# The row sums of the attention weights: once per chunk from a running total on VectorE

## The chip, the cores and the metric

One core of a Trainium2 chip runs the whole program: two transformer layers on a batch of two. Its engines are TensorE (PE; PEld is its weight load), VectorE (DVE), ScalarE (ACT), GpSimd (POOL) and SyncE (SP), which here only starts DMAs. The metric is the device time of one execution in microseconds (us). Three runs of the kernel before had a median of 2285.57 us.

## The reference

```python
# x: (2, 1024, 512) float32; 16 heads of 32 columns; layer 0, then layer 1
xn = layernorm(x)
x = x + attention(xn) + feed_forward(xn)

# attention of one head, causal:
scores = (q_rotated @ k_rotated.T) * 32 ** -0.5        # (1024, 1024), keys after the query masked
pattern = softmax(scores, axis=-1)                     # exp(s - row max) / row sum of these
heads = pattern @ v
out = heads @ Wo.T

# feed-forward: silu(xn @ Wgate.T) * (xn @ Wup.T), then @ Wdown.T
#   2048 hidden columns in layer 0, 1408 in layer 1
```

The row sums are the sums over the keys of the unnormalised weights, exp(score - shift).

## The kernel before

**Tiling.** The 16 heads go in 4 groups of 4. In each layer a group is one turn: a loop body run three times (region `turn0` in layer 0, `turn1` in layer 1) and a fourth, separately written turn (`tail0`, `tail1`). With a batch of two that makes 16 turns: six long turns (layer 0, which carry two pairs of feed-forward chunks), six short turns (layer 1, which carry one pair) and two tails of each layer. A turn has these stages: natural scores (`nat`), from which VectorE takes row maxima; `shift`; the transposed scores and their exponentials; then projection, rotation and DMAs for the next group.

**Scores and weights.** The queries go in two chunks of 512, the keys in blocks of 128. A set is one (chunk, key block): sets 0 to 3 belong to chunk 0, sets 4 to 11 to chunk 1. The last four sets of each chunk are masked and narrow: 512, 384, 256, 128 columns. For each set and each of the four heads, `st` makes scores S<-QS,KS on TensorE (with a second small matmul for the mask) in one of two banks, and ScalarE writes exp of it to `pr`, which has room for two sets. `pv` multiplies the four heads' values with the weights into bank O, and `sums` multiplies a matrix of ones with the same weights into bank E: four matmuls each, on four groups of 32 columns. After a chunk's last `sums`, `heads` copies O and E to SBUF (`heads`, `denom`). Then VectorE takes the reciprocal in two halves (`recip`), scales (`scaled`), ScalarE and GpSimd split the result in a high and a low part (`ah`, `al`), and `wo` multiplies it by the output weights; `add_wo` adds to the residual.

**Order.** `weighted()` writes out the sets: scores of two heads, `pv` of the set before, scores of two heads, `sums` of the set before. `turn()` merges these pieces by hand-written numbers (`FILL`, `LATE`) with pieces of the feed-forward (gate, up, down). The first chunk has none between its sets. Every engine walks the same list of steps and takes its own part of each, in order. So where a step stands in the list is its place in every engine's queue, and a wait at the head of a queue holds all that is behind it. Waits count semaphores: `a_exp` for exponentials, `p_pv` for the weights' last reader, `a_heads` for the copied O and E.

**Where the steps of the second chunk stand.** In a long turn `recip` half 0 follows set 5's first scores and `pv` 4, half 1 and `scaled` follow set 5's last scores, and `wo` stands after `pv` 8. In a short turn both halves and `scaled` stand behind `pv` 5, between the first and the second pair of set 6's scores, and `wo` ahead of set 8. In layer 0's tail half 0 stands ahead of set 6, half 1 and `scaled` ahead of set 7, `wo` behind `pv` 6.

## Time and profile before

| | us |
|---|---|
| three runs, median (lowest to highest) | 2285.57 (2283.03 to 2285.79) |
| profiled execution, span from the first to the last instruction | 2287.4 |
| TensorE busy in it | 2116.6 (93%) |
| VectorE busy | 1159.1 (51%) |
| ScalarE busy | 739.0 (32%) |
| GpSimd busy | 680.0 (30%) |
| mean granted TensorE clock | 0.979 |

The profile has no other time for its own execution than the span. It is 1.8 us above the median of the runs. A busy TensorE is not one at its peak, since matmuls are pipelined and their ends are modelled; starts are better to read than ends. A granted clock of 1.00 is 2.4 GHz, 0.50 is 1.2 GHz.

### The profile page before, as it was taken

What the parts mean: (1) busy time and instruction counts of PE and PEld (TensorE: products, weight loads), DVE (VectorE), ACT (ScalarE), POOL (GpSimd) and SP (SyncE); (2) the same over time, 40 slices, a digit from 0 to 9 for tenths busy, and PEclk for the clock granted to TensorE, in tenths of its full rate; (3) what the DMA queues carried; (4) which work ended last, traced back from release to release, by engine and by line L of the source; (5) the groups of instructions that cost most, each with busy time, mean ns of one, the idle gap of its engine ahead of it and who ended that gap; (6) DMA issues with size and microseconds to landing.
All of it is one profiled execution on the core that took longest, in us unless ns stands there. A gap on an engine that the chain in (4) does not pass through costs nothing.

```text
span 2287.4 us, 35555 instructions
## 1 busy us (share of the span) xinstructions
PE 2116.6 (93%) x11200; PEld 1390.8 (61%) x11200; DVE 1159.1 (51%) x1946; ACT 739.0 (32%) x1357; POOL 680.0 (30%) x428
## 2 busy tenths in 40 slices
PE   4999999999889999999969999999998999999997
PEld 3756656566475656576557566665765756475764
DVE  5534636355445546464356255462645546382733
ACT  3242242423323333423322423324233232424232
POOL 3314323142221414142323142331422314041523
PEclk9999999999999999999979999999998999999998
DMA  3303103141021303040123031130411303030403
GB/s 134 79 29 93 42 22 82 32 111 43 19 73 44 79 28 96 10 115 29 51 101 95 11 93 43 41 85 11 120 34 37 79 20 97 10 96 10 124 21 127
DMA packets 72439, 141.10 MB, mean 62 GB/s; under 512 B 9328, under 2 KB 26736, under 8 KB 71152
## 3 DMA queue, kind: packets, MB, share of 16 engines
q1 hardware_dynamic: 72304, 139.25, 21.9%
q8 instruction: 91, 1.49, 0.3%
q14 instruction: 44, 0.36, 0.1%
HBM read 75.77 MB, written 4.19 MB: 35 GB/s over the span
## 4 chain that ended last, share of the span: by engine, by line
issue 73%; POOL 25%; POOLq 1%; DMA 0%; SPq 0%; ACT 0%
POOL hl L716 5%; POOL swapped L722 4%; POOL pr L728 3%; POOL wgl L693 3%; POOL wul L693 2%; POOL wdl L693 2%; POOL wqkl L693 2%; POOL al L732 2%; POOL raw L709 1%; POOL wol L693 1%; DMA tt<-in_wdown_dram 0%; POOL QS L701 0%; POOLq L715 0%; POOLq L711 0%; POOLq L725 0%
## 5 line engine op out<-in xcount | busy, mean ns | idle before, releaser
L629 ACT ACTIVATE pr<-S 128x512 f32<-128x512 f32 (+3 forms) x768 | 342.2, 489 | 316.5 <-PE S L958 217.2
L847 DVE TENSOR_TENSOR xres<-D,xres 128x512 f32<-128x512 f32 x352 | 242.3, 688 | 370.2 <-PE D L879 364.0
L716 POOL TENSOR_TENSOR hl<-tt,hh 128x512 fp32r<-128x512 f32 x108 | 138.8, 1285 | 872.8 <-ACT hh L653 872.5
L955 PE MATMUL S<-QS,KS 98*128 98x512 f32 (+2 forms) x768 | 267.4, 411 | 19.8 <-ACT pr L629 11.0
L955 PEld LDWEIGHTS S<-QS,KS 98*128 98x128 f32 x768 | 145.1, 192 | 188.3 <-ACT pr L629 165.5
L653 ACT CAST hh<-tt 128x512 fp32r<-128x512 f32 x108 | 67.0, 620 | 488.8 <-DVE tt L861 488.8
L821 DVE TENSOR_REDUCE mp<-S 128x1 f32<-128x128 f32 (+3 forms) x384 | 176.7, 484 | 71.7 <-PE S L937 61.2
L837 DVE RECIPROCAL denom<-denom 128x256 f32<-128x256 f32 x64 | 109.0, 1729 | 186.4 <-ACT denom L636 186.4
L879 PE MATMUL G<-xh,wgh 128*128 128x512 f32 x432 | 180.0, 417 | 19.1 <-issue 13.8
L879 PE MATMUL D<-wdh,hh 128*128 128x512 f32 x432 | 183.8, 426 | 4.1 <-DVE xres L847 3.0
L879 PE MATMUL G<-xh,wgl 128*128 128x512 f32 x432 | 178.2, 412 | 0.0
L879 PE MATMUL U<-xh,wul 128*128 128x512 f32 x432 | 177.3, 410 | 0.0
L879 PE MATMUL G<-xl,wgh 128*128 128x512 f32 x432 | 176.2, 408 | 0.0
L879 PE MATMUL U<-xh,wuh 128*128 128x512 f32 x432 | 174.5, 404 | 0.0
L879 PE MATMUL U<-xl,wuh 128*128 128x512 f32 x432 | 174.4, 404 | 0.0
L879 PE MATMUL D<-wdl,hh 128*128 128x512 f32 x432 | 172.0, 398 | 0.0
L879 PE MATMUL D<-wdh,hl 128*128 128x512 f32 x432 | 171.3, 397 | 0.0
L972 PE MATMUL O<-pr,vh 128*32 128x512 f32 (+3 forms) x1536 | 163.6, 498 | 0.1
L979 PE MATMUL E<-pr,ones 128*32 128x512 f32 (+3 forms) x1536 | 163.4, 497 | 0.0
L858 DVE SCALAR_TENSOR_TENSOR tt<-tt,G 128x512 f32<-128x512 f32 x108 | 73.3, 678 | 125.0 <-ACT tt L647 125.0
L821 DVE TENSOR_REDUCE mp<-O 128x1 f32<-128x512 f32 (+1 forms) x192 | 122.9, 640 | 19.5 <-PE O L934 9.5
L934 PE MATMUL S<-KS,QS 96*128 96x256 f32 (+2 forms) x384 | 121.7, 363 | 9.2 <-DMA QS<-pr 7.5
(145 smaller groups left out, 3794.1 us busy)
## 6 DMA issues: line engine op xcount, KB each, us to landing
KS<-pr SPq DMA_DIRECT2D x192, 128.0 KB, 2.3
QS<-pr SPq DMA_DIRECT2D x192, 128.0 KB, 2.3
raw<-in_wgate_dram SPq DMA_DIRECT2D x29, 512.0 KB, 4.2
raw<-in_wup_dram SPq DMA_DIRECT2D x28, 512.0 KB, 3.7
raw<-in_wdown_dram SPq DMA_DIRECT2D x28, 512.0 KB, 3.5
raw<-in_wqk_dram SPq DMA_DIRECT2D x18, 512.0 KB, 3.5
vh<-val SPq DMA_DIRECT2D x16, 512.0 KB, 3.9
val<-in_x_dram SPq DMA_DIRECT2D x6, 1024.0 KB, 11.0
```

The source lines that it names most:

```text
L629: act.activation(pr[:, (i * HG + h) % 8, skip:W], S[h % 2][:, skip:W], ACT.Exp, scale=SCALE) \
L693: return pool.tensor_tensor(flat(lo), src[:, 0:SIZE[kind]], flat(hi).bitcast(F32), ALU.subtract)
L716: pool.tensor_tensor(hl[:, fc, :], tt[:, (blk * nfc + fc) % 2, :], hh[:, fc, :].bitcast(F32), ALU.subtract) \
L722: pool.tensor_tensor(sw, sw, trig[:, 1, (t % NC) * W:(t % NC + 1) * W], ALU.mult).then_inc(sem["g_sin"], 1)
L821: dve.tensor_reduce(mp[:, h * RT + qb, part:part + 1], NB[(h * len(NAT) + u) % 4][:, 0:w_], AX.X, ALU.max) \
L837: dve.reciprocal(denom[:, half], denom[:, half]).then_inc(sem["v_recip"], 1)
L847: dve.tensor_tensor(xres[:, rt, :], d[:, :], xres[:, rt, :], ALU.add).then_inc(sem["v_dfree"], 1)
L879: ins = pe.matmul(dst, a, b_, start=i == 0, stop=i == len(seq) - 1)
L934: ins = pe.matmul(s[:, 0:wide], QS[0:STACK, h, qb * P:(qb + 1) * P], KS[0:STACK, h, k0:k0 + wide], start=True, stop=not masked)
L955: ins = pe.matmul(s[:, first:W], KS[0:SHIFT, h, kb * P:(kb + 1) * P], QS[0:SHIFT, h, c * W + first:(c + 1) * W], start=True, stop=not masked)
L972: pe.matmul(O[h * DH:(h + 1) * DH, skip:W], vh[:, kb, h * DH:(h + 1) * DH], pr[:, (i * HG + h) % 8, skip:W], start=kb == 0, stop=kb == TPC ...
L979: ins = pe.matmul(E[h * DH:(h + 1) * DH, skip:W], ones[:, :], pr[:, (i * HG + h) % 8, skip:W], start=kb == 0, stop=kb == TPC * (c + 1) - 1)
```

## The change

`sums` is made once per chunk instead of once per set. VectorE keeps a running total `acc` of the four heads' weights. A chunk's first set is the total itself (set 0, whose exponentials are written straight into `acc`) or is copied into it (set 4); each other set is added by one instruction over all four heads (`acc`, eight additions and one copy per turn). TensorE then multiplies the ones with `acc`, 512 columns per head, behind the chunk's last set. `pv` now counts for itself (`p_pv`), the sums have a semaphore of their own (`p_sums`), and an exponential waits for three things: its scores, `pv` of two sets before, and the total's addition of two sets before. `acc` takes the space of two buffers that are unused at that time (`swapped`, `xn`).

```diff
     st = [[[("st", 0, h) for h in two] for two in ((0, 1), (2, 3))]]
     for i in range(1, len(SETS) + 1):
         scores = [("st", i, h) for h in range(HG)] if i < len(SETS) else []
-        now = [scores[:2] + [("pv", i - 1)], scores[2:] + [("sums", i - 1)]]
+        now = [scores[:2] + [("pv", i - 1)], scores[2:]]
+        if i > 1:
+            now[0].append(("acc", i - 1))
         c, kb = SETS[i - 1]
         if kb == TPC * (c + 1) - 1:
-            now[-1].append(("heads", c))
+            now[-1] += [("sums", c), ("heads", c)]
         st.append(now)
     return st
 
     "nat": {"p_nat": 1, "v_max": 1},
     "shift": {"v_chain": 2, "v_m": 1, "p_shift": 1, "v_shift": 1, "d_shift": 32},
     "st": {"p_st": 1, "a_exp": 1},
-    "pv": {},
-    "sums": {"p_pv": 1},
+    "pv": {"p_pv": 1},
+    "acc": {"v_acc": 1},
+    "sums": {"p_sums": 1},
     "heads": {"a_heads": 1},
     "recip": {"v_recip": 1},
     "scaled": {"v_heads": 1, "a_ah": 1, "g_al": 1},
...
-        swapped = sb("swapped", [P, 2, W])
+        acc = sb("acc", [P, HG, W])
+        swapped, xn = acc[:, 0:2, :], acc[:, 2:4, :]
...
             at = n.turns * (2 * PAIRS[1]) + (2 * j + fc)
             return bass.ds(at, 1)
 
+        def weights(i):
+
+            return pr[:, i * HG % 8:i * HG % 8 + HG, :] if i else acc
+
         def proj_bank(n, t):
 
             return S[t % 2] if n.region[:4] == "open" else NB[t]
                 c, kb = SETS[i]
                 skip = max(0, kb - TPC * c) * P
                 act.wait_ge(sem["p_st"], n("p_st", 1))
-                act.wait_ge(sem["p_pv"], n("p_pv"))
-                act.activation(pr[:, (i * HG + h) % 8, skip:W], S[h % 2][:, skip:W], ACT.Exp, scale=SCALE) \
+                later = -1 if h >= 2 else 0
+                act.wait_ge(sem["p_pv"], n("p_pv", later if i else 0))
+                if i:
+                    act.wait_ge(sem["v_acc"], n("v_acc", later if i > 1 else 0))
+                else:
+                    act.wait_ge(sem["p_sums"], n("p_sums"))
+                act.activation(weights(i)[:, h, skip:W], S[h % 2][:, skip:W], ACT.Exp, scale=SCALE) \
                     .then_inc(sem["a_exp"], 1)
 
             def heads_(n, c):
-                act.wait_ge(sem["p_pv"], n("p_pv"))
+                act.wait_ge(sem["p_sums"], n("p_sums"))
                 act.wait_ge(sem["g_al"], n("g_al"))
                 act.copy(heads[:, :], O[:, :])
                 act.copy(denom[:, :], E[:, :]).then_inc(sem["a_heads"], 1)
                 dve.wait_ge(sem["p_shift"], n("p_shift", 1))
                 dve.tensor_copy(mt[:, :], E[0:2 * HG * RT, 0:P]).then_inc(sem["v_shift"], 1)
 
+            def accumulate(n, i):
+                c, kb = SETS[i]
+                skip = max(0, kb - TPC * c) * P
+                dve.wait_ge(sem["a_exp"], n("a_exp", -2 if i < len(SETS) - 1 else 0))
+                if i == 1:
+                    dve.wait_ge(sem["p_pv"], n("p_pv", -1))
+                total_, now = acc[:, :, skip:W], weights(i)[:, :, skip:W]
+                if kb:
+                    dve.wait_ge(sem["v_acc"], n("v_acc"))
+                    ins = dve.tensor_tensor(total_, total_, now, ALU.add)
+                else:
+                    dve.wait_ge(sem["p_sums"], n("p_sums"))
+                    ins = dve.tensor_copy(total_, now)
+                ins.then_inc(sem["v_acc"], 1)
+
             def recip(n, c, k):
                 dve.wait_ge(sem["a_heads"], n("a_heads"))
                 half = slice(k * W // 2, (k + 1) * W // 2)
 
                 pe.wait_ge(sem["a_exp"], n("a_exp", -2 if i < len(SETS) - 1 else 0))
                 for h in range(HG):
-                    pe.matmul(O[h * DH:(h + 1) * DH, skip:W], vh[:, kb, h * DH:(h + 1) * DH],
-                              pr[:, (i * HG + h) % 8, skip:W], start=kb == 0, stop=kb == TPC * (c + 1) - 1)
-
-            def sums(n, i):
-                c, kb = SETS[i]
-                skip = max(0, kb - TPC * c) * P
+                    ins = pe.matmul(O[h * DH:(h + 1) * DH, skip:W], vh[:, kb, h * DH:(h + 1) * DH],
+                                    weights(i)[:, h, skip:W], start=kb == 0, stop=kb == TPC * (c + 1) - 1)
+                ins.then_inc(sem["p_pv"], 1)
+
+            def sums(n, c):
+                pe.wait_ge(sem["v_acc"], n("v_acc"))
                 for h in range(HG):
-                    ins = pe.matmul(E[h * DH:(h + 1) * DH, skip:W], ones[:, :], pr[:, (i * HG + h) % 8, skip:W],
-                                    start=kb == 0, stop=kb == TPC * (c + 1) - 1)
-                ins.then_inc(sem["p_pv"], 1)
+                    ins = pe.matmul(E[h * DH:(h + 1) * DH, :], ones[:, :], acc[:, h, :], start=True, stop=True)
+                ins.then_inc(sem["p_sums"], 1)
 
             def wo_(n, c, i):
                 if c == 0 and i == 0:
```

VectorE's queue in a short turn, after the first chunk: `acc<-pr` and `acc<-acc,pr` are the copy of set 4 and the additions, `heads<-heads,denom` is `scaled`. Before:

```order
L835 ISA
L837 RECIPROCAL denom<-denom 128x256
L835 ISA
L837 RECIPROCAL denom<-denom 128x256
L840 ISA
L841 TENSOR_TENSOR heads<-heads,denom 128x512
L844 ISA
L845 ISA
L847 TENSOR_TENSOR xres<-D,xres 128x512
```

The same place now:

```order
L857 ISA
L858 COPY acc<-pr 128x2048
L849 ISA
L854 ISA
L855 TENSOR_TENSOR acc<-acc,pr 128x2048
L862 ISA
L864 RECIPROCAL denom<-denom 128x256
L862 ISA
L864 RECIPROCAL denom<-denom 128x256
L867 ISA
L868 TENSOR_TENSOR heads<-heads,denom 128x512
```

The copy and set 5's addition have moved in ahead of the reciprocals, and set 6's addition follows the scaling.

ScalarE's queue at the same place: `ah<-heads` stands between the exponentials of set 6's heads 0 and 1 and those of its heads 2 and 3. Before:

```order
L627 ISA
L628 ISA
L629 ACTIVATE pr<-S 128x512
L639 ISA
L640 ISA
L641 CAST ah<-heads 128x512
L627 ISA
L628 ISA
L629 ACTIVATE pr<-S 128x512
```

Now:

```order
L634 ISA
L636 ISA
L638 ISA
L641 ACTIVATE pr<-S 128x512
L651 ISA
L652 ISA
L653 CAST ah<-heads 128x512
L634 ISA
L636 ISA
L638 ISA
L641 ACTIVATE pr<-S 128x512
```

The cast's place is the same; each exponential has one more instruction ahead of it that waits.

## Rows read from the trace of the kernel before

**Rows 1.** The page's busy times of each engine, with share of the span.

```profile
PE 2116.6 (93%) x11200; PEld 1390.8 (61%) x11200; DVE 1159.1 (51%) x1946; ACT 739.0 (32%) x1357; POOL 680.0 (30%) x428
```

**Rows 2.** The row sums: the page's group, then its widest shape (busy us, mean ns).

```profile
L979 PE MATMUL E<-pr,ones 128*32 128x512 f32 (+3 forms) x1536 | 163.4, 497 | 0.0
...
L979 PE MATMUL E<-pr,ones 128*32 128x512 f32 x768 | 102.3, 605 | 0.0
```

**Rows 3.** Who waited for whom: total us, times, longest us.

```profile
PEld S L955 <- ACT pr L629: 165.5, 244, 1.7
```

**Rows 4.** Time line, long turn, second chunk: start, us, engine, line, operation [idle before].

```profile
148.96 3.36 DVE L837 RECIPROCAL denom<-denom 128x256 f32<-128x256 f32 x2 [12.40 <-ACT denom L636]
...
151.99 0.63 PE L955 MATMUL S<-QS,KS 98*128 98x512 f32 x2
...
152.55 1.06 PE L979 MATMUL E<-pr,ones 128*32 128x512 f32 x8
...
153.55 0.50 PE L879 MATMUL D<-wdh,hh 128*128 128x512 f32 x1
...
163.23 0.69 DVE L847 TENSOR_TENSOR xres<-D,xres 128x512 f32<-128x512 f32 x1 [4.03 <-PE D L879]
```

**Rows 5.** Time line, end of the first chunk; then the 384-column exponentials' group.

```profile
144.85 0.73 PE L955 MATMUL S<-QS,KS 98*128 98x512 f32 x2
...
146.19 0.99 PE L955 MATMUL S<-QS,KS 98*128 98x512 f32 x2 [0.24 <-ACT pr L629]
...
L629 ACT ACTIVATE pr<-S 128x384 f32<-128x384 f32 x128 | 55.7, 488 | 46.9 <-PE S L958 46.9
```

**Rows 6.** Time line, short turn: the first chunk's last sums and what follows.

```profile
842.51 0.43 PE L979 MATMUL E<-pr,ones 128*32 128x128 f32 x8
...
844.37 3.37 DVE L837 RECIPROCAL denom<-denom 128x256 f32<-128x256 f32 x2 [18.19 <-ACT denom L636]
...
849.66 0.62 ACT L641 CAST ah<-heads 128x512 fp32r<-128x512 f32 x1
...
854.62 0.50 PE L879 MATMUL D<-woh,ah 128*128 128x512 f32 x1
```

**Rows 7.** Time line, opening: copies with one wait (53.90) and with two (57.61).

```profile
53.47 0.39 PE L879 MATMUL E<-QS,xl 128*128 128x512 f32 x1
...
53.90 0.58 ACT L614 COPY val<-E 128x512 f32<-128x512 f32 x1 [2.13 <-PE E L879]
...
57.11 0.39 PE L879 MATMUL O<-QS,xl 128*128 128x512 f32 x1
...
57.61 0.59 ACT L614 COPY val<-O 128x512 f32<-128x512 f32 x1 [0.34 <-PE O L879]
```

**Rows 8.** Groups of VectorE by form, and two lines with minimum, median and maximum ns.

```profile
L821 DVE TENSOR_REDUCE mp<-S 128x1 f32<-128x128 f32 x128 | 36.4, 284 | 53.7 <-PE S L937 52.9
...
L821 DVE TENSOR_REDUCE mp<-O 128x1 f32<-128x512 f32 x128 | 87.6, 684 | 10.1 <-PE O L934 9.5
...
L841 DVE TENSOR_TENSOR heads<-heads,denom x32: 678/693/1786, 152.4 to 2263.9; 128x512 f32<-128x512 f32 x32
...
L762 DVE CAST QS<-trig x4: 1215/1222/1226, 24.4 to 1757.6; 128x2048 fp32r<-128x2048 f32 x4
```

**Rows 9.** Time line and 1 us windows (TensorE busy, granted clock) between the layers.

```profile
625.84 1.11 PE L888 MATMUL D<-ident,xn 128*128 128x128 f32 x4 [6.05 <-DVE xn L790]
...
627.00:628.00 1.00, 1.00 (x3) 0.50 0.00 0
...
629.00:630.00 1.00, 0.34 (x2) 0.99 0.00 0
...
637.00:638.00 1.00, 0.97 (x5) 0.50 0.00 0
```

**Rows 10.** Time line: GpSimd and VectorE at once.

```profile
879.51 1.65 POOL L722 TENSOR_TENSOR swapped<-swapped,trig 128x512 f32<-128x512 f32 x1 [0.54 <-DVE swapped L808]
...
879.92 1.79 DVE L841 TENSOR_TENSOR heads<-heads,denom 128x512 f32<-128x512 f32 x1
```

More of the change, by code:

```diff
@@ L414, in two_layers @@
         flat_l = [pr[:, 2 * NC * k + NC:2 * NC * (k + 1), :].rearrange("p c n -> p (c n)") for k in range(2)]
-        xn = sb("xn", [P, 2, D])
         heads, denom = sb("heads", [P, W]), sb("denom", [P, W])
@@ L862, in gated @@
                                          ALU.mult, ALU.mult).then_inc(sem["v_h"], 1)
-            walk(dve, dict(v_weights=v_weights, stats=stats, xn=xn_, norm=norm, proj=proj, rotate=rotate, nat=nat, shift=shift,
+            walk(dve, dict(acc=accumulate, v_weights=v_weights, stats=stats, xn=xn_, norm=norm, proj=proj, rotate=rotate, nat=nat, shift=shift,
                            recip=recip, scaled=scaled, add_wo=add_wo, add_down=add_down, gated=gated))
```

## The prediction, made before the changed kernel was run

> **What bounds the kernel now.** The page comes first. TensorE is busy for 93% of the span and VectorE for 51% [rows 1], so work moved from TensorE to VectorE looks free. But these are averages. The groups by shape say what the row sums take: one set of 512 columns (the four heads' matmuls, 8 records) keeps TensorE busy for 102.3 / 96 = 1.07 us, and narrower sets for less. All of them are 163.4 us [rows 2], and two 512-column sets per turn stay where twelve sets stood. The waits decide the rest. TensorE's scores have two banks, so the third score matmul waits for the exponential of the first. Its weight loads were released by that 244 times, for 165.5 us [rows 3], most of it under a matmul still running: the sums are just long enough to cover that ping-pong. What is removed is cover as much as it is work. Last I read the time line of VectorE, ScalarE and TensorE after the first chunk, in a long turn (the loop of layer 0, run six times) and in a short turn (the loop of layer 1, six times) [rows 4 to 6]. That stage decides.
>
> **What a removed sum is worth.** Where other work follows the scores: the score pair starts at 151.99, the sum at 152.55 and the next matmul at 153.55 [rows 4]; two matmuls alone would take 2 x 0.23, so the sum and its bubble cost 1.56 - 0.46 = 1.10 us. Behind masked scores the bubble is smaller; I take 0.93 for 512 columns, 0.71 for 384, 0.50 for 256. Where the next scores follow at once, they wait for ScalarE: pair at 144.85, next scores at 146.19 [rows 5], 1.34 us. That leaves 1.56 - 1.34 = 0.22 us of 1.10. Exponentials of masked sets are shorter, 488 ns at 384 columns [rows 5]: a masked pair with a 512-column sum took 0.82 + 1.00, alone it waits 0.70 + 0.49 + 0.07, so 0.56 is left, and by the same sum 0.32 and 0.21 for the narrower sets.
>
> Each exponential has a third wait now (scores, values, running total), handled one after the other. No row shows three. One against two is shown once: a copy with one wait began 0.43 us after the start of its last matmul, with two 0.50 us [rows 7]. I take 0.07 us for each half set without cover; the ends are 0 and 0.15, 0 to 15 us over 16 turns with some six such halves.
>
> **What VectorE gets.** Per turn eight additions and one copy. The trace has no addition of 2048 columns. Reduces of 128 and 512 columns take 284 and 684 ns, 1.04 ns a column, and the addition of 512 columns from SBUF has a median of 693 ns [rows 8]: 693 + 1536 x 1.04 = 2.29 us, and 1.76, 1.22 and 0.69 for the narrower sets. The other end is 4 x 0.69 = 2.77 us. The copy is nearest to the cast of 2048 columns, 1.22 us [rows 8], at worst 2.29. Together 4 x 2.29 + 2 x 3.67 + 1.2 = 17.7 us per turn, 284 us in all. VectorE rises from 51 to some 63%, which bounds nothing by itself. (The table of the Trainium skill, "VectorE: DVE Perf Modes", section "The perf-mode tier table", gives 2293 ns for the addition and 1227 ns for the copy; by it the sum is the same.)
>
> **The first chunk** has no other work between its sets in either turn. Removed are 0.56 + 0.32 + 0.21; the last half saved there goes, since the one remaining sum is 512 columns wide (1.00) where the removed one had 128 (0.36), and the added waits take 0.2 to 0.3. Net gain 0.2 us per turn. The additions hide under VectorE's 12.4 us of idle time before the reciprocal [rows 4].
>
> **Long turns, second chunk.** The copy (1.2 us) fits between the last exponential and the arrival of `denom`, so the reciprocals start as before. TensorE has down projections between the sets, and an addition of 2.29 us plus two of 0.69 (3.7 us) fits: VectorE was idle for 4.03 us ahead of the add at 163.23 [rows 4]. Four sums go before the output projection: 1.10 + 0.15 + 1.10 + 0.93 = 3.3, with bubbles 3.7 us by laying the pieces end to end. Behind it go 0.93 + 0.71; the sum of the 256-column set goes too, but the values then wait for the last exponential (0 gained), and the last sum widens from 128 to 512 columns (0.6 lost), 0.3 for waits behind GpSimd's weight split. Net 0.7. A long turn gains 0.2 + 3.7 + 0.7 = 4.6 us; six give 28 us.
>
> **Short turns, second chunk: the new wait.** Before, VectorE starts the reciprocals at 844.37 (3.37 us), scales the heads behind them, ScalarE casts `ah` at 849.66, in its queue behind the exponentials of set 6's first two heads and ahead of those of the other two, and that is in time [rows 6]. Now set 5's addition stands on VectorE ahead of both reciprocals, and it waits for set 5's last exponential. Times from the end of the chunk's sums: gate/up work to 1.9, scores of set 5 to 3.9, its exponentials end at 5.2, addition to 7.5, reciprocals to 10.9, scaling to 11.6, cast to 12.3. Behind the cast wait the exponentials of set 6's heads 2 and 3, and behind these set 7's scores: 13.0. TensorE has nothing from 7.1 to 13.0, 5.9 us. It reaches the output projection at 15.2, before at 854.6 against the sums' end at 842.51 + 0.36, 11.8 [rows 6]: +3.4 us, though two sums are gone. From there to the chunk's last sums the four removed ones are nearly all uncovered (0.45, 0.56, 0.32 and 0 are gained) and the wide last sum and its wait for the addition cost 1.2, the waits 0.3: +0.2.
>
> Then the clock. After TensorE had stood still from 619.79 to 625.84 (6.05 us) its granted clock was 0.50, 1.2 GHz of 2.4, until 629, 3.2 us of work later [rows 9]. The new pause is as long. 3.2 us at half speed is 1.6 us; part of it lies under ScalarE, so 1.3. (The Trainium skill, "TensorE: Matmul & The Clock Gate", section "What's actually happening", says that an idle array falls to 1.2 GHz and sustained activity brings 2.4 back; the trace agrees.) A short turn: -0.2 + 3.4 + 0.2 + 1.3 = +4.7 us, six +28 us.
>
> **Tails.** In layer 0's, set 5's addition stands between the reciprocals and set 6's behind the scaling. Laid out as above: first reciprocal to 4.9, addition to 7.6, second reciprocal and scaling to 10.0, cast to 10.7. There VectorE's next addition has begun (10.1 to 12.4), and GpSimd's `al` waits for it: when GpSimd's operation started at 879.51 and VectorE's of 512 columns at 879.92, they took 1.65 and 1.79 us instead of 1.29 and 0.69 [rows 10]. (The Trainium skill, "SBUF — State Buffer", section "Who interferes with whom": the pair of ports that the two share is held for a whole instruction; here that turns one wait of 0.69 into one of 2.29.) `al` at 13.7, against 11.1 for the same pieces with their sums laid end to end (2 x 0.95, four halves of 1.65, 0.95, 1.65): +2.6, clock +1.3, removed sums behind it -1.6, first chunk -0.2: +2.1 each, +4. Layer 1's tail has other work in nearly every half and its reciprocals early: 3 x 1.10 + 2 x 0.93 + 0.71 + 0.50 - 0.6, less 1 us because the next gate waits for a product queued behind an addition: -5 each, -10.
>
> **Sum.** -28 + 28 + 4 - 10 = -6 us on the profiled span of 2287.4, 1.8 above the median of 2285.57: 2280 us.
>
> **Rivals.**
> (a) Slower: the clock falls in the first chunk of every turn too. With the sums gone, TensorE works 0.5 to 0.6 us of 1.2 to 1.3 in three halves. For it: after 629, four transposes with pauses around them were enough for a second fall, still there at 637 [rows 9]. Against: the same ping-pong today leaves the clock up in most turns. Price 16 x 1.7 = +27: 2307 us. It decides once seven turns show it. 0.20.
> (b) Slower: the copy takes 2.29 us and the additions 2.77, so that reciprocals and what waits for them come 1.1 to 1.6 us later; 16 x 1 = +16, 2297 us. Against: the cast of 2048 columns at 1.22 us. 0.08.
> (c) Faster: the short turns' block is only half as long, because the queue of ScalarE is less full than I laid out, and the clock holds: +28 becomes about 0, 2252 us. For: most of it is my end-to-end laying. Against: the order on both queues is fixed. 0.18.
> (d) Faster: TensorE is the bound everywhere and a removed sum is worth its full 1.10, 0.93 and so on: 9.9 us a turn less 2.1 for the two that stay, 125 us in 16 turns, less the new waits (32): 2193 us. Against: 244 loads released by ScalarE. 0.07.
> The balance above: 0.47, own range 2270 to 2291.
>
> A measurement of this kernel tells 0.2%, 4.6 us, from no change. The balance is faster than that 0.26, within 0.18 and slower 0.03; with (c), (d) faster 0.51; with (a), (b) slower 0.31. The range from 2248 to 2308 leaves out (d) and a little at the other end.
>
> **What would show it.** Right: in each short turn two reciprocals start some 5 us later behind a 2.29 us addition, TensorE pauses 5 to 6 us ahead of set 7's scores at 0.50 clock after it; a long turn is some 4.6 us shorter; E<-acc,ones x256 is near 34 us busy. Wrong: short turns that are no longer than before; additions far from 2.29; long turns that gain under 3 us; a clock of 0.50 in first chunks.

## The result, and the profile after

The changed kernel takes 2311.49 us, median of 4 runs (2309.96 to 2317.16), beside 2285.68 us for the kernel before (4 runs). The ratio is 1.0121, 95% interval 1.0107 to 1.0136: slower by 1.2%, 26 us. Forecast were 2280 us and, most likely, faster.

The page's busy times, then groups by shape (times, busy us, mean ns of one), and who waited for whom:

```profile
PE 2050.7 (89%) x9920; PEld 1384.8 (60%) x9920; DVE 1446.8 (63%) x2122; ACT 748.8 (32%) x1357; POOL 695.8 (30%) x428
```

```profile
L855 DVE TENSOR_TENSOR acc<-acc,pr 128x2048 f32<-128x2048 f32 x64 | 151.9, 2373 | 58.1 <-ACT pr L641 58.1
L1006 PE MATMUL E<-acc,ones 128*32 128x512 f32 x256 | 43.3, 756 | 3.7 <-DVE acc L855 3.7
L858 DVE COPY acc<-pr 128x2048 f32<-128x2048 f32 x16 | 19.6, 1225 | 39.6 <-PE E L1006 34.5 <-ACT pr L641 5.1
```

```profile
PEld S L982 <- ACT pr L641: 212.2, 287, 6.1
PE S L982 <- ACT pr L641: 86.0, 111, 5.6
```

VectorE rose to 63%, as laid out [rows 1]. The row sums take TensorE 43.3 us where they took 163.4 [rows 2]; 34 were forecast, but some ran at half clock, 1062 ns each instead of 617. TensorE's busy time fell by 66 us only, since other matmuls became longer: the scores take 297.2 us by the page, before 267.4. And the loads of the scores' weights wait 212 us for ScalarE where it was 165.5 [rows 3], and the longest wait is 6.1 us instead of 1.7. That is the pause of the short turns. Their time line (start, us, engine, line, operation, idle before) has it where the forecast put it [rows 6]:

```profile
836.38 1.23 DVE L858 COPY acc<-pr 128x2048 f32<-128x2048 f32 x1 [3.69 <-PE E L1006]
836.52 0.59 ACT L647 COPY heads<-O 128x512 f32<-128x512 f32 x1 [1.15 <-PE E L1006]
842.74 2.29 DVE L855 TENSOR_TENSOR acc<-acc,pr 128x2048 f32<-128x2048 f32 x1 [5.13 <-ACT pr L641]
844.95 3.36 DVE L864 RECIPROCAL denom<-denom 128x256 f32<-128x256 f32 x2
...
849.21 0.62 ACT L653 CAST ah<-heads 128x512 fp32r<-128x512 f32 x1 [5.20 <-DVE heads L868]
849.73 1.08 ACT L641 ACTIVATE pr<-S 128x512 f32<-128x512 f32 x2
850.37 1.28 PE L982 MATMUL S<-QS,KS 98*128 98x512 f32 x2 [5.63 <-ACT pr L641]
```

The reciprocals start 8.4 us behind the copy of `heads` (836.52), not 1.1 us behind it; the cast stands ahead of two exponentials in ScalarE's queue, and TensorE's next scores behind those.

TensorE's clock in the same turn, in the last windows of the first chunk and around that pause (window, length, TensorE busy and records, granted clock, DMA share, GB/s):

```profile
825.00:827.00 2.00, 1.51 (x12) 1.00 0.00 0
827.00:829.00 2.00, 1.48 (x13) 1.00 0.46 162
829.00:831.00 2.00, 1.98 (x16) 1.00 0.26 100
831.00:833.00 2.00, 1.61 (x10) 0.59 0.00 0
833.00:835.00 2.00, 2.00 (x11) 0.50 0.00 0
...
837.00:839.00 2.00, 2.00 (x8) 0.71 0.00 0
...
846.00:848.00 2.00, 0.00 (x0) 1.00 0.00 0
848.00:850.00 2.00, 0.00 (x0) 0.60 0.00 0
850.00:852.00 2.00, 1.63 (x6) 0.50 0.00 0
```

The second fall, behind the pause, was forecast. The first, in the first chunk, was rival (a). From about 838 on the clock is back at 1.00 until the pause, so each turn pays twice.

To see where the time went, I cut every turn of a profiled run at three marks on ScalarE's time line: its first exponential, the copy of the first chunk's `heads`, that of the second's. "Rest" runs from there to the next first exponential, and is counted with the turn that follows it. Mean us per turn:

```
                          short turns (6)          long turns (6)
                          first second  sum        first second  sum
before                    15.5  28.1   43.6        14.8  41.9   56.7
changed kernel            17.3  36.0   53.3        15.9  38.3   54.2
forecast difference       -0.2  +4.9   +4.7        -0.2  -4.4   -4.6
measured difference       +1.9  +7.9   +9.8        +1.1  -3.6   -2.5
```

Six short turns cost 59 us. Six long turns give back 15 in their chunks and, unforecast, 23 in the rest. Layer 0's tails add 6, those of layer 1 give 4. With 1.5 less in the short turns' rest that is +21 us, the difference of the profiled spans (2287.4 and 2308.2). Eleven of sixteen first chunks have the low clock; before it was one, right behind the opening of layer 1.

The unforecast 23 us are mostly a pause that has gone. Where the loop of layer 0 starts its second and third turn, four times in the batch of two, TensorE stood still in the kernel before, with nothing named that it waited for, and 3.4 us at half speed followed (rest 86.8, now 81.7); now its weight load waits 0.27 us. First a row of the kernel before, then its counterpart:

```profile
215.39 0.49 PE L879 MATMUL G<-xh,wgh 128*128 128x512 f32 x1 [3.71 <-issue]
```

```profile
206.85 0.19 PEld L906 LDWEIGHTS G<-xh,wgh 128*128 128x128 f32 x1 [0.27 <-issue]
```

One of the two DMA queues that carry instructions, q8 (packets, MB, share), marks the place. In the kernel before it brings nine packets between 205 and 345 us, one passage of the loop, and three of them from 209 to 217, around the pause:

```profile
q8 instruction: 9, 0.15, 0.5%
q8 instruction: 3, 0.05, 3.2%
```

In the changed kernel it brings none between 205 and 345 us (q14, the other one, brings six of 8 KB there and none in the kernel before). So where the pause stands, q8 brings instructions again in each passage of the loop, and where it has gone it does not.

### The profile page after: what moved, and what is told of

The parts are those of the page before. It is cut to its first block, busy times and chain, and to the rows that moved or that the text cites. A ratio compares the mean times of both kernels' runs of the same rounds, so it can differ in the third digit from the quotient of the medians.

```text
span 2308.2 us, 34341 instructions
## 1 busy us (share of the span) xinstructions
PE 2050.7 (89%) x9920; PEld 1384.8 (60%) x9920; DVE 1446.8 (63%) x2122; ACT 748.8 (32%) x1357; POOL 695.8 (30%) x428
## 4 chain that ended last, share of the span: by engine, by line
issue 72%; POOL 26%; POOLq 1%; DMA 0%; SPq 0%; ACT 0%
POOL hl L728 5%; POOL acc L734 4%; POOL pr L740 3%; POOL wgl L705 3%; POOL wul L705 2%; POOL wdl L705 2%; POOL al L744 2%; POOL wqkl L705 2%; POOL raw L721 2%; POOL wol L705 1%; DMA tt<-in_wdown_dram 0%; POOL QS L713 0%; POOLq L727 0%; POOLq L723 0%; POOLq L737 0%
## 5 line engine op out<-in xcount | busy, mean ns | idle before, releaser
L855 DVE TENSOR_TENSOR acc<-acc,pr 128x2048 f32<-128x2048 f32 (+3 forms) x160 | 273.2, 1708 | 257.1 <-ACT pr L641 257.1
L641 ACT ACTIVATE pr<-S 128x512 f32<-128x512 f32 (+3 forms) x704 | 315.3, 480 | 273.3 <-PE S L985 140.3
L982 PE MATMUL S<-QS,KS 98*128 98x512 f32 (+2 forms) x768 | 297.2, 440 | 92.8 <-ACT pr L641 86.0
L982 PEld LDWEIGHTS S<-QS,KS 98*128 98x128 f32 x768 | 151.9, 200 | 238.7 <-ACT pr L641 212.2
L999 PE MATMUL O<-pr,vh 128*32 128x512 f32 (+3 forms) x1408 | 155.1, 515 | 14.8 <-ACT pr L641 14.8
L744 POOL TENSOR_TENSOR al<-heads,ah 128x512 fp32r<-128x512 f32 x32 | 46.1, 1439 | 315.5 <-ACT ah L653 315.5
L833 DVE TENSOR_REDUCE mp<-E 128x1 f32<-128x512 f32 (+1 forms) x192 | 114.1, 594 | 10.5 <-PE E L964 10.4
```

The lines of the kernel that those rows point to most:

```text
L641: act.activation(weights(i)[:, h, skip:W], S[h % 2][:, skip:W], ACT.Exp, scale=SCALE) \
L744: pool.tensor_tensor(al[:, :], heads[:, :], ah[:, :].bitcast(F32), ALU.subtract).then_inc(sem["g_al"], 1)
L833: dve.tensor_reduce(mp[:, h * RT + qb, part:part + 1], NB[(h * len(NAT) + u) % 4][:, 0:w_], AX.X, ALU.max) \
L855: ins = dve.tensor_tensor(total_, total_, now, ALU.add)
L982: ins = pe.matmul(s[:, first:W], KS[0:SHIFT, h, kb * P:(kb + 1) * P], QS[0:SHIFT, h, c * W + first:(c + 1) * W], start=True, stop=not masked)
L999: ins = pe.matmul(O[h * DH:(h + 1) * DH, skip:W], vh[:, kb, h * DH:(h + 1) * DH], weights(i)[:, h, skip:W], start=kb == 0, stop=kb == TPC ...
```

## The experiments

All ratios are to the kernel before, with 95% intervals. In the expectations the short turns' second chunk is split at the first matmul of the output projection. That split read 12.2 and 15.9 us for the kernel before. With all records it is 11.4 and 16.7 (the changed kernel 17.6 and 18.4); the sum is the same 28.1.

### No additions, one sum per chunk

```diff
 def accumulate(n, i):
+    return                       # and no wait for v_acc anywhere
```

> As the changed kernel, but VectorE adds nothing (the copy and the eight additions are left out, the row sums are formed once per chunk from what stands in the tile, so the output is not the reference's); each exponential waits for two things again. Theory 1 (VectorE's queue): the short turns' middle stretch (18.0 us in the changed kernel, 12.2 before) falls to 11 to 12.5, the pause of TensorE ahead of set 7 is gone, and their end stretch goes from 18.3 to about 16; the clock still falls in the first chunk (stretch of 16.5 to 16.9 us), since that is TensorE's missing sums. Time 2311 - 6 x (6 + 2.3) - some 6 in tails = 2255 us. Theory 2 (lost cover alone): the stretches after stay within 1 us of the changed kernel's, 2300 us or more.

Measured: 2225.15 us, 0.9735 (0.9721 to 0.975). Short turns 15.6 + 26.6 us, long turns 15.6 + 37.5. Four first chunks of sixteen had a low clock, mostly long turns, none short. So theory 1 holds for the short turns' block and 2 falls: without VectorE's part the change would save 60 us (some 20 of them the vanished pause), with it it costs 26.

One part of the expectation failed. The clock was to fall in the first chunks for want of the sums, and in the short turns it fell in none of six (15.6 us where 16.5 to 16.9 were expected). Over the 11.8 us from a short turn's first exponential TensorE is busy for 10.99 us in the kernel before, for 10.08 here, and for 9.67 in the changed kernel, ahead of the fall that comes in all six. So the missing sums alone do not bring it about there. The 15.2 us of a long first chunk at full clock are no measure of the sums' worth: this edit lets the wide sum wait for set 4's exponentials, 0.83 us in which TensorE stands still, and in the changed kernel it does not wait.

### Additions beside all the old sums

```diff
-        now = [scores[:2] + [("pv", i - 1)], scores[2:]]
+        now = [scores[:2] + [("pv", i - 1)], scores[2:] + [("each", i - 1)]]
```

> The kernel before with VectorE's copy and eight additions beside TensorE's sums of every set: the row sums come from TensorE as before, what VectorE adds up is not used. Theory 1 (VectorE's queue): the short turns' middle stretch grows from 12.2 to 17 or 18 us as in the changed kernel, though TensorE keeps every sum; first chunks keep the clock at 1.00 (14.8 and 15.2 us), long turns keep their length and their pause at the loop's start (rest 86.8). Time 2286 + 6 x 5.5 + some 6 in tails = 2325 us. Theory 2 (the slowdown comes from the sums taken away): no stretch moves by more than 1 us, 2290 us.

Measured: 2339.87 us, 1.0234 (1.0216 to 1.0253). VectorE's time line after a short turn's first chunk:

```profile
847.35 0.59 ACT L648 COPY heads<-O 128x512 f32<-128x512 f32 x1
847.67 1.23 DVE L860 COPY acc<-pr 128x2048 f32<-128x2048 f32 x1 [2.52 <-ACT pr L642]
852.43 2.29 DVE L857 TENSOR_TENSOR acc<-acc,pr 128x2048 f32<-128x2048 f32 x1 [3.54 <-ACT pr L642]
854.64 3.35 DVE L866 RECIPROCAL denom<-denom 128x256 f32<-128x256 f32 x2
...
858.90 0.62 ACT L654 CAST ah<-heads 128x512 fp32r<-128x512 f32 x1 [4.94 <-DVE heads L870]
```

`heads` to cast is 11.6 us, in the changed kernel 12.7, and no sum was taken from TensorE here. Short turns take 15.8 + 35.4 us, so the second chunk's growth of 7.3 us is there with all sums kept. Theory 1 holds for it, theory 2 falls. Only one of sixteen first chunks lost its clock, so the additions and the third waits alone do not bring the fall about either. The time was 15 us over the 2325 expected. The long turns did not keep their length, though: their pause at the loop's start has gone (rest 81.8), with TensorE's matmuls as many as before.

### Set 5's addition behind the scaling

```diff
+    if name == "turn1":
+        late = [[s for s in p if s != ("acc", 5)] + [("acc", 5)] * (("scaled", 0) in p) for p in late]
```

> As the changed kernel, but in the short turns set 5's addition stands behind the two reciprocals and the scaling on VectorE, not ahead of them. Theory 1 (queue order): reciprocals start at once behind the heads, the cast is 3 to 5 us earlier, the pause ahead of set 7 goes and with it the low clock: middle stretch from 18.0 to 12.5 or 13, time 2311 - 6 x 5.2 = 2280 us. Theory 2 (the stretch is long because the clock is low from the first chunk on and each exponential is dearer): it stays above 16 us, 2303 us or more.

Measured: 2273.65 us, 0.9943 (0.9928 to 0.9958): 38 us less than the changed kernel, by the place of one instruction in six turns. That it is already below the kernel before it owes to the vanished pause, some 20 us.

```profile
834.70 0.59 ACT L649 COPY heads<-O 128x512 f32<-128x512 f32 x1 [1.15 <-PE E L1008]
835.81 3.36 DVE L866 RECIPROCAL denom<-denom 128x256 f32<-128x256 f32 x2
839.21 0.69 DVE L870 TENSOR_TENSOR heads<-heads,denom 128x512 f32<-128x512 f32 x1
840.86 2.29 DVE L857 TENSOR_TENSOR acc<-acc,pr 128x2048 f32<-128x2048 f32 x1 [0.96 <-ACT pr L643]
842.02 0.61 ACT L655 CAST ah<-heads 128x512 fp32r<-128x512 f32 x1
```

`heads` to cast is 7.3 us instead of 12.7 (6.4 in the kernel before). The second chunk fell from 36.0 to 29.6, 6.4 us a turn, 38 us in all: theory 1, and a little more than it said, for the low clock behind the pause went too. The first chunks kept their low clock (17.5 us), so it is a cost of its own.

### Two waits in front of each exponential

```diff
 # the addition waits for its set's values product; the exponential for the addition alone
-                act.wait_ge(sem["p_pv"], n("p_pv", later if i else 0))
+                dve.wait_ge(sem["p_pv"], n("p_pv", 0 if i < len(SETS) - 2 else -1))
```

> As the changed kernel, but each exponential waits for two things, as before the change: an addition now waits for its set's values product, so the exponentials of the set after next need only the addition. If the third wait is what sets the 0.45 us between the starts of two short exponentials (0.30 before): pairs start 0.30 apart again, first chunk -0.4 us, end stretch of short turns -0.7 us and the clock falls in fewer first chunks, 2311 - 16 x 1 = 2295 us or less. If it is something else (sums' cover alone): 2309 to 2313.

Measured: 2317.99 us, 1.0143 (1.0128 to 1.0158), no gain. A long first chunk at full clock takes 14.5 us for 15.1, 0.07 us per half, and pairs start 0.30 apart again. It is also 0.3 us shorter than with all its sums (14.8): that is what the removed sums are worth there, less the wide one. Eight first chunks of sixteen have the low clock, not eleven. But the additions now come behind the values product and the second chunks lose more: 39.0 for 38.3 us in long turns, 37.0 for 36.0 in short ones. Expected was 2295; the wait's price was right and the conclusion wrong, since this edit moved the additions later as well.

### A third wait in the kernel before

```diff
                 act.wait_ge(sem["p_pv"], n("p_pv"))
+                act.wait_ge(sem["v_rope"], n("v_rope"))
```

> The kernel before with one more wait in front of every exponential, for a semaphore that has long been reached; nothing else changes. The variant with two waits had first chunks of 14.5 us at full clock where the changed kernel has 15.1: 0.56 us in 8 halves, 0.07 us a half. If the third wait costs that wherever it stands: first chunks +0.5 us (15.3 and 15.7), end stretches +0.5 to +1.0, 16 x 1.2 = +19 us, 2305 us; if TensorE's sums cover it: 2286 to 2289. The pause at the start of the long turns' loop (3.7 us in the kernel before, in none of the five variants so far): it stays if it comes from the length of TensorE's program, which is untouched here (rest 86.8); it goes (rest 81.8) if it hangs on where the other engines' instructions lie.

Measured: 2286.62 us, 1.0007 (0.9998 to 1.0016), 11 runs. By the time alone the wait would be free. By the trace it is not: first chunks 15.4 and 15.5 us (+0.6 and, against a short turn at full clock, +0.3), short second chunks 28.5 for 28.1. The pair of narrow exponentials shows it. In the kernel before two of them take 0.58 us together, the second starting 0.30 us after the first:

```profile
869.85 0.58 ACT L629 ACTIVATE pr<-S 128x128 f32<-128x128 f32 x2 [0.61 <-PE S L958]
```

With the third wait they start 0.45 us apart:

```profile
861.14 0.28 ACT L630 ACTIVATE pr<-S 128x128 f32<-128x128 f32 x1 [0.47 <-PE S L959]
861.59 0.28 ACT L630 ACTIVATE pr<-S 128x128 f32<-128x128 f32 x1 [0.17 <-issue]
```

What hid it in the profiled execution (2282.35 us) is that the pause at the long loop's start stood in one place of four, 15 us less. The other ten have no trace, and where they had the pause is not known. So that pause is not fixed to the old sums, nor to the length of TensorE's program.

### The change in long turns and layer 1's tail alone

```diff
+MODES = {'turn0': '01', 'tail0': '', 'turn1': '', 'tail1': '01'}   # chunks added up by VectorE
```

> The change made in the long turns and in layer 1's tail alone; the short turns and layer 0's tail are as before the change. Each kind of turn should keep its own length: six long turns as in the changed kernel (about 136.5 for 143.5 us where the loop's start pause goes, 3.9 less in the first of each batch), tail of layer 1 some 1 to 3 us shorter, short turns 43.3 us of weighted stretches instead of 53.2. 2286 - 34 - 4 = 2248 us. Rival: the long turns' gain was borrowed from what follows, or the pause at the loop's start comes back with the short turns' old code: 2268 us or more.

Measured: 2243.07 us, 0.9817 (0.9804 to 0.9829). Short turns are back at 15.2 + 28.1. The long turns keep 15.4 + 38.4 and a rest of 81.3. The gain was not borrowed; the rival falls.

### Only their second chunk

```diff
+MODES = {'turn0': '1', 'tail0': '', 'turn1': '', 'tail1': '1'}
```

> The same two kinds of turn, and there only the second chunk (eight sets) is added up by VectorE; the first chunk keeps TensorE's sums. If the low clock in the first chunk comes from its missing sums, it stays at 1.00 there (14.8 us instead of 15.1 to 16.5) and the middle stretch of every long turn is 22.0 to 22.2, not 22.9: 6 us less than the variant with both chunks, 2241 us. If the clock falls anyway, both are equal within 2 us.

Measured: 2232.67 us, 0.9777 (0.9765 to 0.979), 10 us less than the run above (6 were expected). All first chunks have the full clock, long ones 14.8 us, and their second chunks 37.4, with none of the scatter (37.7 to 39.0) that they had with a low clock ahead of them in five first chunks of sixteen.

### All turns, first chunk as before the change

```diff
+MODES = {'turn0': '1', 'turn1': '1', 'tail0': '1', 'tail1': '1'}
```

> The changed kernel in all turns, but its first chunk has TensorE's sums of every set as before. If the clock falls in first chunks for want of the sums: stretches of 14.8 and 15.2 us again (16.5 and 16.9 in the changed kernel), the clock 1.00 in them; the block of the short turns stays (middle 17.5 to 18). 12 x 1.6 + 4 x 0.2 = 20 us less than 2311: 2291 us. If the lower clock belongs to the additions of the second chunk or to the third wait, first chunks stay above 16 us: 2308 us.

Measured: 2281.51 us, 0.9987 (0.9978 to 0.9995): 30 us less than the changed kernel where 20 were expected. The edit takes the additions and the third wait out of the first chunk too. No first chunk has the low clock. A short turn's, from 3 us behind its first exponential:

```profile
815.00:817.00 2.00, 1.26 (x10) 1.00 0.00 0
817.00:819.00 2.00, 1.92 (x13) 1.00 0.00 0
819.00:821.00 2.00, 2.00 (x20) 1.00 0.20 72
821.00:823.00 2.00, 2.00 (x22) 1.00 0.49 190
823.00:825.00 2.00, 2.00 (x23) 1.00 0.00 0
```

Where the changed kernel has TensorE busy for 1.5 us of 2, the sums make it 1.92 to 2.00. First chunks give 19 of the 28 us between the two profiled spans. The second chunks give most of the rest (long 38.3 to 37.4, short 36.0 to 35.3): they no longer begin at half speed.

### Where the tiles lie

```diff
+MODES = {'turn0': '', 'turn1': '', 'tail0': '', 'tail1': ''}
```

> Every instruction of the kernel before in its order, with only what the change did around it: the tiles `swapped` and `xn` lie in the 128x2048 tile `acc`, and two semaphores more exist (one more step each at SyncE's start). If the changed kernel's gain of 5.1 us at each of the four loop starts of the long turns came from where things lie: the pause goes here too, 2286 - 20 = 2266 us. If the pause comes by chance from execution to execution with TensorE's program at its old length (the kernel with a third wait had it in one of four places): 2275 to 2286, two to four pauses. If it belongs to TensorE's instructions alone: 2285.

Measured: 2286.63 us, 1.0007 (0.9997 to 1.0017). The pause is there in all four places:

```profile
215.40 0.79 PE L921 MATMUL G<-xh,wgh 128*128 128x512 f32 x1 [3.81 <-issue]
358.43 0.63 PE L921 MATMUL G<-xh,wgh 128*128 128x512 f32 x1 [3.23 <-issue]
```

Shared tiles and the new semaphores cost nothing and are not what took the pause away. The queue q8 goes with it. From the DMA view (packets, MB, share), this kernel, as the kernel before:

```profile
q8 instruction: 91, 1.49, 0.3%
```

In the kernel with a third wait it was 65 with one pause, in all others 50 to 56 with none. (Where a rest is 83.1 us instead of 81.5, in four variants, the clock was low for 3.4 us late in it; no pause and no more packets go with that.)

### The last two sets on TensorE

```diff
+        late = new and i - 1 >= len(SETS) - 2      # sets 10, 11: sums_old behind ("sums", c)
```

> The variant with VectorE's sums in the second chunk of the long turns and layer 1's tail (2232.7 us), but the two narrowest sets, 10 and 11, are summed by TensorE behind the one sum of the tile, so that the chunk's end waits for no addition. Theory: the last sums stood 1.24 us behind the last exponential (addition and signal); TensorE pays 0.64 + 0.40 for the two sums, but the wide one (1.0) now lies where TensorE waited for ScalarE. End stretch of long turns 15.4 to 14.7, tail 29.3 to 28.6: 8 x 0.7 = 5.6, 2227 us. Rival: that stretch is bound by TensorE's work, the end is longer by the two sums: +0.6 x 8, 2238 us.

Measured: 2227.39 us, 0.9742 (0.973 to 0.9755), the best version that computes the reference. Long turns end 0.2 us earlier, the tail 0.3 (where its clock stayed up), less than the 0.7 expected: the last narrow sum is paid in full behind the last exponential, and in the long turns `heads` is copied 2.8 us behind it where it was 3.1. That makes 2 us in all. The medians of the two variants are 5.3 us apart, but their profiled spans only 1.1 (2228.9 and 2230.0), so most of the difference is not explained by this.

```profile
316.24 0.28 ACT L657 ACTIVATE pr<-S 128x128 f32<-128x128 f32 x1 [0.17 <-issue]
...
318.41 0.43 PE L1024 MATMUL E<-pr,ones 128*32 128x128 f32 x8
319.05 0.59 ACT L663 COPY heads<-O 128x512 f32<-128x512 f32 x1 [2.53 <-PE E L1024]
```

### Both mends in all turns

```diff
+MODES = {'turn0': '1', 'turn1': '1', 'tail0': '1', 'tail1': '1'}   # and ("acc", 5) behind ("scaled", 0)
```

> All turns with VectorE's sums in the second chunk, TensorE's in the first, and in the short turns set 5's addition behind the scaling: the two mends that each helped alone, together. If clock and queue order are separate costs, they add up: short turns 15.2 + 11.4 + 18.0 instead of 15.2 + 16.8 + 18.4 us, 2281.5 - 6 x 5.8 = 2247 us. If the low clock behind the pause did the harm and not the order, less than half of that: 2265 or more. The short turns should stay 1.3 us each over those of the kernel before (28.1 us from heads to heads), for the end stretch waits for ScalarE and for the last addition.

Measured: 2250.59 us, 0.9835 (0.9817 to 0.9853). Short turns 15.3 + 29.5 us: the first chunk and the queue order are separate costs and nearly add up (2247 were expected). 1.4 us a turn stay over the old 28.1 in the second chunk: its middle stretch is 10.3 us for 11.4, its end stretch 19.2 for 16.7. In that end stretch the clock falls in all six short turns, and in four of them it stays low for over 3 us of what follows, which is 1.2 us longer on average. With set 5's addition moved and all else as in the changed kernel the end stretch was 18.0 us at full clock, in five turns of six.

### TensorE's program made long again, twice

```diff
+                if n.region == "turn0":
+                    for _ in range(5 if k < GU_PARTS - 1 else 3):
+                        pe.wait_ge(s_const, 8)
```

> The changed kernel with 81 more instructions on TensorE in the loop of the long turns, all of them waits for a semaphore reached at the program's start, between feed-forward matmuls: the loop's program is as long again as before the change (1416 instructions by the built program, 1413 before, 1335 in the changed kernel). If the pause at the loop's start comes from that length: rest of the second and third long turns 86 to 87 us instead of 81.8, some 40 more packets on the queue that carries instructions (50 in the changed kernel, 91 before), 2311 + 4 x 5.1 = 2331 us. If it hangs on something else in the kernel before: no pause, 50 to 56 packets, 2311 to 2316 us.

> The variant without additions (2225 us; output not the reference's, as there) with the same 81 satisfied waits on TensorE in the loop of the long turns: TensorE 1416, ScalarE 245, VectorE 259 instructions in that loop (1413, 241, 259 in the kernel before, which pauses in four loop starts of four; 1416, 289, 293 in the run before this, which pauses in none). If the pause needs TensorE's long program beside the short ones of the other two: rest of the second and third long turns 86 to 87 us, about 90 packets on the instruction queue, 2225 + 20 = 2245 us. If program length has no part in it: 50 to 56 packets, 2225 to 2230 us.

Measured: 2314.96 us, 1.0127 (1.011 to 1.0144), and without additions 2230.25 us, 0.9774 (0.9749 to 0.9798). Neither has the pause: rests 81.3 to 81.7, once 83.2, and 50 instruction packets in both. The number of instructions alone does not bring it back, so both theories of program length fall. What takes the pause away stays open.

## Why the prediction was wrong

The step that failed is the first chunk. It was put at a net gain of 0.2 us a turn, with the clock kept at 1.00; measured were +1.9 us in short turns and +1.1 in long ones, and all first chunks together +18 us for -3, which is 21 of the 27 us between the forecast and the measured balance of the span (-6 and +21). Two terms of the short turns' second chunk were too small besides. Much of the rest came out as laid out.

**Prices of VectorE: right.** The additions take 2.29 us where nothing disturbs them (forecast 2.29), on average 2.37; the copy takes 1.22 (1.22). Rival (b) is out (its 16 us make 2296, not 2297).

**The block in the short turns: right in kind, too small.** Order and place came out as laid out: pause of 5.6 us (5.9), half speed behind it. Forecast were +3.4 and +1.3 for the clock, 4.7. Moving one addition gave back 6.4 us, and with all the old sums kept the additions lengthened the second chunk by 6.9 (35.4 against 28.5 with the third wait alone). The clock term took 3.2 us of work at low clock; behind the pause the changed kernel works some 4.7 us at half speed, in scores, values and output projection, and another 1.6 us at the chunk's start, left over from the first chunk's fall.

**The first chunk: the step that failed.** Two terms were to give +0.2 us: the removed sums less the wide one 0.45, the waits -0.2 to -0.3, and the clock nothing. In a long turn at full clock the sums gave 0.3 and the waits took 0.56, so the chunk grew by 0.2 us instead (14.83 to 15.06). Then the clock: with it low a long first chunk takes 16.5 us, 1.45 more. This is rival (a), given 0.20, and its condition held: eleven turns of the sixteen, seven were asked for. Its price was 1.7 us each. With the first chunk as before the change the span was 28 us shorter. In short turns, taking the sums away beside the additions lengthens the turn by 2.1 us (51.2 to 53.3), and taking them away without the additions shortens it by 1.1 (43.3 at full clock to 42.2). The forecast kept 1.00 because the old ping-pong did; but that ping-pong had the sums in it [rows 5]. I had written that what is removed "is cover as much as it is work" and then priced only the work. The runs show that neither the missing sums alone (0 of 6 short first chunks, though 4 of the other 10) nor the additions and third waits alone (1 of 6) bring the fall, but both together do (6 of 6). What tips it is open: with two waits and additions TensorE was busy for 10.01 of the same 11.8 us in a short turn that kept the clock and in one that lost it.

**The added wait: right in price, too few of them counted.** 0.07 us per half, from one row each [rows 7], stands in two experiments at some 0.56 us in the eight halves of a long first chunk. What was missed is that it does not fall only on the few halves without cover: it shows there even with the sums in place (15.4 for 14.8; in short turns 15.5 for 15.2).

**The chunk's end in short turns: sized too small.** The forecast had +0.2; measured were 18.4 us for 16.7, and 18.0 with set 5's addition moved, +1.3 at full clock. Its costs were right: from the start of the last exponential to the copy of `heads` it is 2.5 us, before 1.2 (addition of 0.69 us and wide sum, 1.2 laid out), and the third wait alone lengthens the stretch by 0.3. What failed is the gain: the four removed sums were counted as 1.33 us, and only some 0.3 came. Without additions the stretch takes 16.4 us, so more came there; which wait takes it away stays open.

**Long turns: 4.6 forecast, 2.5 measured in the chunks.** The second chunk gave 3.6 where 4.4 were laid out. At full clock and with the first chunk kept it gives 4.5, so the working was right, and the difference goes with the first chunk, whose low clock reaches into the second. The extra 3.8 us a turn in the rest were not in any step. They come from the vanished pause, some 20 us of the balance. Without that luck the change would have cost about 46 us.

**Tails.** Layer 0's +3 each (forecast +2.1), layer 1's -2.2 (-5): there one of two first chunks lost the clock; the other tail gave 3.4 us. In layer 0's the split by GpSimd waited for the addition as laid out [rows 10]: it took 2.52 us where it took 1.28 before, and TensorE stood still for 3.46 us until it was done.

```profile
561.73 2.28 DVE L855 TENSOR_TENSOR acc<-acc,pr 128x2048 f32<-128x2048 f32 x1
...
562.62 2.52 POOL L744 TENSOR_TENSOR al<-heads,ah 128x512 fp32r<-128x512 f32 x1 [6.71 <-ACT ah L653]
```

The product queued behind an addition, for which 1 us was taken off, was not looked at.

So the sum failed on the short turns (+59 us for +28), and the vanished pause, which the forecast had not seen, hid that it failed on the long ones too (-15 in their chunks for -28, -38 with the rest).

## What to carry to other kernels

Before work is taken from an engine that waits in a ping-pong, ask of each piece whether it lies under the other engine's time: if so, its removal gains little, and with new waits beside it it cost the clock here. When an engine gets new work, list what stands behind each new instruction in its queue up to the next result that another engine waits for. Here one addition behind two reciprocals instead of ahead of them was worth 38 us, more than the change lost. Apply such a change per stage, and keep it where the stage has other work between the sets: in the second chunks of long turns and layer 1's tail it gives 2.2% (2.6% with the last two sets on TensorE; in both some 0.9% is the vanished pause), everywhere it costs 1.2%.

## What the runs showed of the hardware

With all sums in place, TensorE's clock stayed at 1.00 in every first chunk of six variants and fell in one of 16 in two more kernels (the one before, and the one with the additions beside the sums). It fell to 0.50 in 4 and 2 of 16 without sums and additions (the second with the longer program), and in 11, 13 and 12 of 16 where additions and third waits came on top. The same code gave both: long first chunks at 15.06 and at 16.5 us in one run. An addition of 512 columns took 0.69 us alone and 1.03 when it started while GpSimd split weights (a long turn with the change in its second chunk alone):

```profile
315.32 2.36 POOL L720 TENSOR_TENSOR wgl<-raw,wgh 128x1024 fp32r<-128x1024 f32 x1 [4.77 <-ACT wgh L683]
...
317.20 1.03 DVE L870 TENSOR_TENSOR acc<-acc,pr 128x512 f32<-128x512 f32 x1 [2.30 <-ACT pr L655]
```

The Trainium skill, "SBUF — State Buffer", section "Who interferes with whom", says that a VectorE instruction with two inputs in SBUF contends with a GpSimd one that reads it. The rows agree: 0.34 us of delay, within the 0.48 that GpSimd still had to run.

The "issue" pause of 3.1 to 3.8 us where a loop jumps back, with some ten more packets of q8 for each, was wholly unexpected. It was there in four places of four in two programs, once in a third with the same TensorE matmuls, and never in the others, one of which has these matmuls too (the additions beside all sums). In these others q8 brings at most one packet during the loop's second and third passage, in the first two nine each time, and in the third program eight in the one passage with the pause and at most one in the others. No run here settles what sets it. A packet is 16.4 KB on average (1.49 MB in 91). The Trainium skill, "Advanced Engine Details and Errata", section "ISA Cache", gives lines of 16 KB, 256 instructions, and 128 KB of them for TensorE; the size of a packet agrees, and by an estimate from these figures a loop of some 1400 instructions (six lines of 16 KB) would fit. By that the pause needs another reason than the loop's length, as the last two runs found.
